# First layer of a two-layer model on one core: expert choice, prefix sums, positions and scatter issued one batch later, layer norm ahead of the squares

## The chip, the core and the metric

The kernel runs on 1 of the 8 cores of a Trainium2 chip. The metric is the device time of one execution in microseconds. Three executions of the kernel before took 2236.86, 2238.84 and 2248.63 us, median 2238.84. The engines are TensorE (PE; PEld is its weight load), VectorE (DVE), ScalarE (ACT), GpSimd (POOL) and SyncE (SP, which here only issues DMAs).

## What is computed

```python
xn = layernorm(x)                                   # x: 16 x 512 x 128, float32
x  = x + linear_attention(xn) + moe(xn)             # first layer
xn = layernorm(x)
x  = x + chunked_softmax_attention(xn) + rwkv_ffn(xn)   # second layer
...
# moe: 8 experts, top 2 of the softmax of xn @ router_w.T, weights renormalised,
# each expert relu(x @ w_fc.T)**2 @ w_proj.T, plus one shared MLP of the same form
# linear_attention: rope, phi = elu + 1, causal: num_t = q_t (sum_{s<=t} k_s v_s), divided by q_t sum k_s
```

The program computes its first-layer attention by blocks of 128 tokens: masked scores inside a block, sums of k v for the blocks before.

## The kernel before, in words

The first layer is a software pipeline over 16 batches of 512 tokens (`over_batches`: two batches written out, a hardware loop of six rounds with two batches each, two written out). Each engine has its own `body(b, first, last)`, and the engines meet by semaphores. Nothing plans the order: it is the order of the calls in those bodies. In body b the engines do the attention of batch b in four slices of four heads (`scores`, `evac_s` on ScalarE and `cut` on VectorE with `mask` on GpSimd, `attend`), the output of batch b-1 (`turn_y`, `project_out`, `residual`), the front of batch b+1 (`turn_xn`, `project_qk`, `rotate`, `project_v`, `turn_k`, `sum_states`, `states`), and the layer norm of batch b+2 (`ln_moments`, `ln_sqrt`, `ln`).

The choice of experts belongs to the front: for batch b+1, in body b,

- `router` (VectorE, L863 to L896): maximum of the logits, difference, exponential on ScalarE (`exp_router`, L620), sum, rank of each expert by comparing all pairs, `pickb` (top two) for TensorE, the two weights. 17 small operations, each waiting for the one before;
- `prefix` (TensorE, L1401): 14 small matmuls that count, for each token, the tokens before it that chose each expert, into bank W6;
- `slots` (VectorE, L909 to L925): the weights divided by their sum, the row of each choice from the counts and the running `fill`, as integers in `idx`;
- `store_route` (SP, L363 and L365): weights and rows to DRAM;
- `scatter` (GpSimd, L513): 8 indirect DMAs that write the rows of xn of the batch to the experts' queues in DRAM. For batch b they are issued in body b, three after the masks of slice 0, three after those of slice 1, two after those of slice 2.

The places that matter below:

- `ln` (L809 to L824) ends body b on VectorE, behind `square_h` and `slots`. Its last four operations write xn of batch b+2, and wait until the scatters of batch b have landed, since they read the same buffer.
- `turn_xn` (L1361) transposes xn into W6, which is shared by `turn_xn`, `turn_y`, `project_qk`, `project_v`, `turn_k`, `prefix` and `shared_fc`.
- `turn_oT(b, 0)` (L1483) waits for `residual` of batch b-1 (L962, semaphore xa_ready), since both use bank W7.
- `project_qk(b+1, 0)` (L1377) waits for the copy of yT on ScalarE (L630).
- `relu_h` (L636) on ScalarE and `square_h` (L957) on VectorE follow the four `shared_fc` matmul groups (L1505), two buffers each.

After the last batch VectorE makes a plan of tiles of 256 rows (L1036 to L1056), and the experts' tiles run, then the second layer. Both are the same before and after.

Of the kernel before, what the change touches and what calls it, by code (L numbers as in the profile page):

```python
# [16 lines left out]
NB = FF // 128  # L17
# [77 lines left out]
def build(nc, io, out):  # L95
    ctx = ExitStack()
    with ctx:
# [198 lines left out]
        def early(b, d):  # L296

            return b.less(d)
# [34 lines left out]
        def _(sp):  # L333
# [43 lines left out]
            def body(b, first, last):  # L377
                if not (b.known() is not None and b.known() + 2 >= B):
                    load_x(b + 2)
                if not first:  # L380
                    store_xa(b + -1)
                load_xr(b)
                if not last:
                    store_route(b + 1)

            store_route(Turn(0, 0))
            over_batches(sp, body)
# [101 lines left out]
        def _(pool):  # L489
# [27 lines left out]
            def body(b, first, last):  # L517
                for s in range(SHEETS):
                    for g in COPIED:
                        mask(b, s, g)  # L520
                    if s < SHEETS - 1:
                        scatter(b, range(3 * s, min(3 * s + 3, 2 * J)))

# [57 lines left out]
        def _(act):  # L581
# [69 lines left out]
            def front(n):  # L651
                exps(n)
                sheets_of_k(n)
                evac_v(n)
                evac_ktok(n)
                exp_router(n)

            def body(b, first, last):
                if not first:
                    evac_oT(b + -1, 3)  # L660
                evac_s(b, 0)
                if not last:
                    evac_xnT(b + 1)
                evac_s(b, 1)
                if not first:
                    evac_yT(b + -1)
                evac_oT(b, 0)
                evac_s(b, 2)
                if not last:
                    exps(b + 1)  # L670
                evac_oT(b, 1)
                if not last:
                    sheets_of_k(b + 1)
                evac_s(b, 3)
                if not last:
                    evac_v(b + 1)
                evac_oT(b, 2)
                if not last:
                    evac_ktok(b + 1)
                    exp_router(b + 1)  # L680
                if not (b.known() is not None and b.known() + 2 >= B):
                    ln_sqrt(b + 2)
                for k in range(NB):
                    relu_h(b, k)
# [105 lines left out]
        def _(dve):  # L790
# [174 lines left out]
            def front(n):  # L965
                rotate(n, 0)
                rotate(n, 1)
                feature(n)
                logits_out(n)
                states(n)  # L970
                router(n)
                slots(n)

            def body(b, first, last):
                cut(b, 0)
                if not first:
                    y_out(b + -1, 3)
                    normalise(b + -1)
                cut(b, 1)
                if not last:  # L980
                    rotate(b + 1, 0)
                cut(b, 2)
                if not first:
                    residual(b + -1)
# [12 lines left out]
                if not last:  # L997
                    states(b + 1)
                    router(b + 1)
                y_out(b, 2)  # L1000
                for k in range(NB):
                    square_h(b, k)
                if not last:
                    slots(b + 1)
                if more:
                    ln(b + 2)

# [344 lines left out]
        def _(pe):  # L1352
# [3 lines left out]
            def turn_xn(n, first_layer=True):  # L1356
                pe.wait_ge(xn_ready, n.at(J, J))
                if first_layer and not early(n, 1):
                    pe.wait_ge(prefix_read, n.at(1, 0))
                for j in range(J):  # L1360
# [3 lines left out]
            def project_qk(n, c):  # L1364
# [8 lines left out]
                else:  # L1373
                    pe.wait_ge(rot_cos, n.at(2, 1))
                    pe.wait_ge(rot_sin, n.at(2, 1))
                rhs = xnT[n.p][:, 1:T + 1]
                pe.matmul(W5[:, :], wqk[:, 2 * c, :], rhs, start=True, stop=True).then_inc(qk_ps, 1)  # L1377
# [12 lines left out]

            def prefix(n):

                pe.wait_ge(picked, n.at(1, 1))
                if early(n, 1):
                    pe.wait_ge(ktok_sb, n.at(1, 1))
                else:
                    pe.wait_ge(h_relu, n.at(NB, 0))
                for j in range(J + 1):
# [87 lines left out]
            def turn_y(b, last):  # L1486
                pe.wait_ge(y_ready, b.at(1, 1))
                if last:
                    pe.wait_ge(prefix_read, B)
                    pe.wait_ge(h_relu, b.at(NB, NB))  # L1490
                else:
                    pe.wait_ge(xnT_sb, (b + 2).at(1, 1))
# [5 lines left out]
            def shared_fc(b, k, last):  # L1498
# [4 lines left out]
                else:  # L1503
                    pe.wait_ge((state_sb, yT_sb)[k], (b, b + -1)[k].at(1, 1))
                pe.matmul((W5, W6)[k % 2][:, :], sfc[:, k * 128:(k + 1) * 128], xnT[b.p][:, 1:T + 1], start=True, stop=True).then_inc(fc_ps, 1)  # L1505
# [14 lines left out]
            def body(b, first, last):  # L1520
# [12 lines left out]
                if not first:  # L1533
                    project_out(b + -1)
                turn_oT(b, 0)
                if not last:
# [12 lines left out]
                for k in range(NB):  # L1549
                    shared_fc(b, k, last)  # L1550
                if not last:
                    prefix(b + 1)

# [7 lines left out]
            sum_states(n0)  # L1561
            prefix(n0)
            over_batches(pe, body)
# [276 lines left out]
```

## Time and profile before

| what | value |
| --- | --- |
| median of three executions | 2238.84 us |
| the profiled execution, its own time | 2259.64 us |
| its span (first to last instruction) | 2257.9 us |
| mean granted clock of TensorE | 0.812 |
| PE busy, share of the span | 1797.4 us, 80% |
| DVE busy | 1331.0 us, 59% |
| ACT busy | 938.0 us, 42% |
| POOL busy | 501.7 us, 22% |

The first layer takes the time up to about 775 us. A group of the profile's rows gives the start in us, the duration in us, the engine, the line of the kernel, the operation with its output and inputs (names of the program, `t`, `P`, `bank` stand for several buffers), the shape, and in brackets the idle time of the engine before it and who ended it. A granted clock of 1.00 is 2.4 GHz and 0.50 is 1.2 GHz. Durations of matmuls overlap, since they are pipelined: a group of 32 matmuls at 451.89 of 1.17 us ends where the next begins.

### The profile page before, as it was taken

What the parts mean: (1) busy time and instruction counts of PE and PEld (TensorE: products, weight loads), DVE (VectorE), ACT (ScalarE), POOL (GpSimd) and SP (SyncE); (2) the same over time, 40 slices, a digit from 0 to 9 for tenths busy, and PEclk for the clock granted to TensorE, in tenths of its full rate; (3) what the DMA queues carried; (4) which work ended last, traced back from release to release, by engine and by line L of the source; (5) the groups of instructions that cost most, each with busy time, mean ns of one, the idle gap of its engine ahead of it and who ended that gap; (6) DMA issues with size and microseconds to landing.
All of it is one profiled execution on the core that took longest, in us unless ns stands there. A gap on an engine that the chain in (4) does not pass through costs nothing.

```text
span 2257.9 us, 40845 instructions
## 1 busy us (share of the span) xinstructions
PE 1797.4 (80%) x13376; PEld 1062.4 (47%) x13376; DVE 1331.0 (59%) x3305; ACT 938.0 (42%) x1675; POOL 501.7 (22%) x517
## 2 busy tenths in 40 slices
PE   2788788888888699996478797777877778777796
PEld 1455455555555499996133343333433333333332
DVE  2666666665665444443565676666766666766563
ACT  2334334433443133332135454444544445444453
POOL 1443343344334111113211101111011110110000
PEclk9799989989988799998557876777767777677776
DMA  3010101011000366664333322233221332222200
GB/s 77 28 40 25 32 30 35 25 33 35 27 24 26 90 207 210 210 209 139 78 71 72 73 56 58 43 76 72 59 56 41 76 75 62 50 42 63 62 7 10
DMA packets 116987, 152.65 MB, mean 68 GB/s; under 512 B 29012, under 2 KB 81364, under 8 KB 112212
## 3 DMA queue, kind: packets, MB, share of 16 engines
q1 hardware_dynamic: 102920, 119.73, 21.7%
q0 software_dynamic: 13952, 31.48, 4.7%
q8 instruction: 61, 1.00, 0.2%
q14 instruction: 54, 0.44, 0.1%
HBM read 109.53 MB, written 41.62 MB: 67 GB/s over the span
## 4 chain that ended last, share of the span: by engine, by line
PE 56%; DVE 21%; DMA 9%; issue 8%; ACT 4%; SPq 1%; DVEq 0%; POOL 0%; POOLq 0%; ACTq 0%
PE bank L1640 7%; PE bank L1471 6%; PE bank L1594 6%; DVE nmax L1128 6%; PE bank L1585 6%; PE bank L1664 6%; DMA shift_d<-shift 5%; PE bank L1456 3%; PE bank L1453 3%; PE bank L1437 3%; PE bank L1516 3%; DMA QT<-shift_d 2%; PE bank L1483 2%; PE bank L1615 2%; PE bank L1377 2%
## 5 line engine op out<-in xcount | busy, mean ns | idle before, releaser
L1128 DVE TENSOR_REDUCE nmax<-bank 128x1 f32<-128x512 f32 (+3 forms) x704 | 432.5, 630 | 173.9 <-PE bank L1640 160.4
L733 ACT ACTIVATE P<-bank 128x512 f32<-128x512 f32 x640 | 369.0, 598 | 382.2 <-PE bank L1664 375.8
L1640 PE MATMUL bank<-KT,QT 76*128 76x512 bf16 (+3 forms) x1024 | 336.7, 389 | 107.7 <-DVE nmax L1128 84.6
L1664 PE MATMUL bank<-QT,KT 78*128 78x512 bf16 (+3 forms) x1024 | 318.8, 395 | 129.8 <-DMA QT<-shift_d 125.3
L1640 PEld LDWEIGHTS bank<-KT,QT 76*128 76x128 bf16 x1024 | 98.9, 114 | 337.9 <-DVE nmax L1128 286.4
L505 POOL TENSOR_TENSOR P<-P,tri 128x512 f32<-128x512 f32 x128 | 160.2, 1271 | 416.9 <-ACT P L643 416.7
L1664 PEld LDWEIGHTS bank<-QT,KT 78*128 78x128 bf16 x1024 | 117.4, 120 | 236.6 <-issue 113.7
L1471 PE MATMUL bank<-P,V 128*32 128x512 f32 (+3 forms) x2048 | 227.9, 529 | 0.0
L565 POOL DMA_DIRECT2D out<-xr x16 | 13.2, 822 | 740.9 <-DVE xr L1280 740.9
L1077 DVE TENSOR_TENSOR hT<-hr 128x512 f32<-128x512 f32 x144 | 99.6, 692 | 109.6 <-ACT hr L704 109.6
L704 ACT ACTIVATE hr<-bank 128x512 f32<-128x512 f32 x144 | 86.0, 597 | 167.6 <-PE bank L1585 167.6
L1594 PEld LDWEIGHTS bank<-P,hT 128*128 128x128 f32 x1152 | 140.4, 192 | 3.8
L544 POOL DMA_INDIRECT hT<-ys_d,idx x128 | 125.0, 977 | 76.4 <-issue 71.5
L1594 PE MATMUL bank<-P,hT 128*128 128x128 f32 x1152 | 140.5, 275 | 0.0
L1585 PE MATMUL bank<-P 128*128 128x256 f32 x576 | 139.9, 387 | 0.5 <-ACT P L699 0.5
L513 POOL DMA_INDIRECT xs_d<-xn,idx x128 | 126.6, 989 | 32.4 <-issue 32.0
L1361 PE MATMUL bank<-ident,xn 128*128 128x128 f32 x128 | 32.6, 404 | 113.4 <-DVE xn L824 113.4
L939 DVE COPY yb<-bank 128x144 f32<-128x144 f32 x128 | 38.5, 301 | 142.4 <-PE bank L1483 140.9
L626 ACT COPY oT<-bank 128x512 f32<-128x512 f32 x128 | 75.0, 586 | 101.5 <-PE bank L1456 60.4
L1456 PE MATMUL bank<-P,V 128*32 128x128 f32 x2048 | 116.8, 303 | 0.0
L1585 PEld LDWEIGHTS bank<-P 128*128 128x128 f32 x576 | 106.0, 194 | 12.8 <-ACT P L699 0.9
L530 POOL DMA_DIRECT2D ys_d<-P x72 | 52.2, 725 | 259.7 <-DVE P L1083 248.5
(207 smaller groups left out, 2750.6 us busy)
## 6 DMA issues: line engine op xcount, KB each, us to landing
P<-in_fc SPq DMA_DIRECT2D x72, 256.0 KB, 2.6
P<-in_proj SPq DMA_DIRECT2D x72, 256.0 KB, 2.9
QT<-parts_d SPq DMA_DIRECT2D x96, 192.0 KB
parts_d<-parts SPq DMA_DIRECT2D x32, 384.0 KB, 2.6
P<-xs_d SPq DMA_DIRECT2D x72, 128.0 KB, 2.2
ys_d<-P POOLq DMA_DIRECT2D x72, 128.0 KB, 2.7
KT<-parts_d SPq DMA_DIRECT2D x64, 128.0 KB
KT<-parts_d SPq DMA_DIRECT2D x32, 192.0 KB
```

The source lines that it names most:

```text
L505: nc.gpsimd.tensor_tensor(blocks, blocks, tri[:, :, :], ALU.mult).then_inc(a_masked, 1)
L513: nc.gpsimd.indirect_dma_start(xs_d[:, :], bass.IndirectOffsetOnAxis(ap=idx[n.p][:, k:k + 1], axis=0), xn[n.p][:, k % J, :], None).then_in ...
L544: nc.gpsimd.indirect_dma_start(ya[n.p][:, k, :], None, ys_d[:, :], bass.IndirectOffsetOnAxis(ap=idx[n.p][:, k:k + 1], axis=0)).then_inc(ga ...
L733: nc.scalar.activation(P[s % 2][:, u, :], bank[k % 2][:, :], ACT.Exp, scale=float(DH) ** -0.5).then_inc(s_sb, 1)
L1077: nc.vector.tensor_tensor(hT[:, t.p % 2, 2 * k:2 * k + 2, :], h, h, ALU.mult).then_inc(e_sq, 1)
L1128: nc.vector.tensor_reduce(nmax[:, j, h:h + nh], bank[2 + k % 2][:, 0:nh * w].rearrange("p (h w) -> p h w", h=nh), AX.X, ALU.max, negate=Tr ...
L1456: ins = pe.matmul(OT[32 * g:32 * g + 32, tile], V[b.p][:, j, G * s + g, :], P[s % 2][:, g, tile], start=(j == 0), stop=True, skip_group_ch ...
L1471: ins = pe.matmul(OT[32 * g:32 * g + 32, 128 * kb:T], V[b.p][:, kb, G * s + g, :], P[s % 2][:, u, c:c + n], start=(k == 0), stop=(k == J - ...
L1585: ins = pe.matmul(w[:, i * GT:(i + 1) * GT], wfc[t.p][:, c * 128:(c + 1) * 128], xgT[t.p % 2], start=True, stop=True)
L1594: ins = pe.matmul(bank[6 + t.p % 2][:, c * 128:(c + 1) * 128], hT[:, t.p % 2, k, c * 128:(c + 1) * 128], wpj[t.p][:, k, :], start=(k == 0) ...
L1640: ins = pe.matmul(bank[2 + k % 2][:, i * w:(i + 1) * w], QT[n.p][0:MROWS, h, j * 128:(j + 1) * 128], KT[n.p][0:MROWS, h, 0:w], start=True, ...
L1664: ins = pe.matmul(bank[k % 2][:, c:c + n], KT[b.p][0:SROWS, h, 128 * kb:128 * kb + 128], QT[b.p][0:SROWS, h, 128 * kb:T], start=True, stop ...
```

## The change

Everything of the expert choice of batch b+1 that stood in body b now stands in body b+1, and is written with b. On VectorE `router(b)` comes behind `cut(b, 1)`, `slots(b)` behind `cut(b, 2)` and ahead of `residual(b-1)`; on ScalarE `exp_router(b)` behind `evac_s(b, 1)`; on TensorE `prefix(b)` behind `project_out(b-1)`; on SP `store_route(b)` behind `load_xr(b)`; on GpSimd all 8 scatters behind the masks of slice 2. `ln(b+2)` moves up, behind `states(b+1)`, ahead of the last `y_out` and the squares. On ScalarE `evac_ktok(b+1)` now precedes `evac_oT(b, 2)`. Waits for bank W6 are rewritten for the new order. No arithmetic changes.

```diff
@@ SP
                 load_xr(b)
-                if not last:
-                    store_route(b + 1)
-
-            store_route(Turn(0, 0))
+                store_route(b)
@@ POOL
                     for g in COPIED:
                         mask(b, s, g)
-                    if s < SHEETS - 1:
-                        scatter(b, range(3 * s, min(3 * s + 3, 2 * J)))
+                    if s == SHEETS - 2:
+                        scatter(b, range(2 * J))
@@ ACT, front and body
                 evac_ktok(n)
-                exp_router(n)
...
                 evac_s(b, 1)
+                exp_router(b)
                 if not first:
                     evac_yT(b + -1)
...
-                evac_oT(b, 2)
                 if not last:
                     evac_ktok(b + 1)
-                    exp_router(b + 1)
+                evac_oT(b, 2)
@@ DVE, front and body
                 states(n)
-                router(n)
-                slots(n)
...
                 cut(b, 1)
+                router(b)
                 if not last:
                     rotate(b + 1, 0)
                 cut(b, 2)
+                slots(b)
                 if not first:
                     residual(b + -1)
...
                     states(b + 1)
-                    router(b + 1)
+                if more:
+                    ln(b + 2)
                 y_out(b, 2)
                 for k in range(NB):
                     square_h(b, k)
-                if not last:
-                    slots(b + 1)
-                if more:
-                    ln(b + 2)
@@ PE
             def turn_xn(n, first_layer=True):
                 pe.wait_ge(xn_ready, n.at(J, J))
-                if first_layer and not early(n, 1):
-                    pe.wait_ge(prefix_read, n.at(1, 0))
+                if first_layer and not early(n, 2):
+                    pe.wait_ge(h_relu, (n + -1).at(NB, 0))
+                elif first_layer and not early(n, 1):
+                    pe.wait_ge(ktok_sb, n.at(1, 0))
...
                     pe.wait_ge(rot_sin, n.at(2, 1))
+                    if not early(n, 1):
+                        pe.wait_ge(prefix_read, n.at(1, 0))
...
-            def prefix(n):
+            def prefix(n, last):
                 pe.wait_ge(picked, n.at(1, 1))
-                if early(n, 1):
-                    pe.wait_ge(ktok_sb, n.at(1, 1))
+                if not last:
+                    pe.wait_ge(rot_sin, (n + 1).at(2, 1))
                 else:
-                    pe.wait_ge(h_relu, n.at(NB, 0))
+                    pe.wait_ge(yT_sb, n.at(1, 0))
...
                     project_out(b + -1)
+                prefix(b, last)
                 turn_oT(b, 0)
...
                     shared_fc(b, k, last)
-                if not last:
-                    prefix(b + 1)
```

TensorE before, from the last shared matmuls of one batch into the next (`ident,xn` is turn_xn, `pickb` prefix, `P,QT` scores, `sfc` shared_fc, `oT` turn_oT):

```order
L1505 MATMUL bank<-xnT,sfc 128x512 [waits h_relu] x2
L1401 MATMUL bank<-pickb,before 128x8 [waits h_relu,picked]
L1401 MATMUL bank<-pickb,before 128x8 x13
L1437 MATMUL bank<-P,QT 128x128 [waits a_sb,a_cut,phi,k_sheets]
L1437 MATMUL bank<-P,QT 128x128 x15
L1483 MATMUL bank<-ident,oT 128x128 [waits y_sb,oT_sb]
L1483 MATMUL bank<-ident,oT 128x128 x3
L1361 MATMUL bank<-ident,xn 128x128 [waits prefix_read,xn_ready]
```

TensorE after, in the middle of a batch, from the end of project_out (`wo,yT`) to the attention of slice 1; prefix now stands here, and nothing stands between the shared matmuls and the scores:

```order
L1514 MATMUL bank<-wo,yT 128x128
L1399 MATMUL bank<-pickb,before 128x8 [waits rot_sin,picked]
L1399 MATMUL bank<-pickb,before 128x8 x13
L1481 MATMUL bank<-ident,oT 128x128 [waits xa_ready,y_sb,oT_sb]
L1481 MATMUL bank<-ident,oT 128x128 x3
L1375 MATMUL bank<-xnT,wqk 128x512 [waits prefix_read,rot_sin,rot_cos]
L1376 MATMUL bank<-xnT,wqk 128x512
```

The prefix matmuls moved from the end of the batch before to between project_out and turn_oT, and wait there for the choice and for the first rotation of the next batch.

VectorE after, from the cut of slice 2 to the copy of the first outputs:

```order
L931 TENSOR_TENSOR P<-bank,tri 128x512 [waits a_ps]
L906 TENSOR_SCALAR psum_<-psum_ 128x4
L907 RECIPROCAL psum_<-psum_ 128x4 [waits slots_step]
L911 TENSOR_TENSOR wts<-p,psum_ 128x8 [waits slots_step]
L916 TENSOR_TENSOR pos<-bank,fill 128x32 [waits prefix_read,prefix_ps]
L918 TENSOR_TENSOR fill<-fill,bank 128x8 [waits slots_step]
L919 TENSOR_TENSOR prod<-pick,pos 128x64
L921 TENSOR_REDUCE slotf<-prod 128x8 [waits slots_step]
L922 CAST idx<-slotf 128x8 [waits slots_step]
L959 TENSOR_TENSOR xr<-xr,bank 128x512 [waits xr_loaded0,proj_ps]
L936 COPY yb<-bank 128x4x36 [waits oTT_ps]
```

Slots moved in between the cut and the residual, and its middle waits for the prefix matmuls of the same batch.

## Rows read from the trace of the kernel before

**Rows 1.** Waits of PE, 94 to 715 us: total, times, longest.
```profile
PE bank L1361 <- DVE xn L824: 47.4, 12, 4.2
```
**Rows 2.** Stretches: length, PE, PEld, DVE, ACT, POOL busy, then PEclk, DMA, GB/s.
```profile
94.60:714.50 619.90, 524.07 (x5562) 349.20 (x5558) 389.44 (x1029) 249.05 (x432) 250.28 (x224) 0.91 0.10 30
...
721.30:724.60 3.30, 1.23 (x34) 1.03 (x33) 3.20 (x7) 1.50 (x4) 2.96 (x3) 1.00 0.05 5
724.70:728.10 3.40, 3.40 (x24) 1.95 (x24) 1.03 (x2) 0.66 (x2) 2.77 (x4) 0.50 0.15 43
```
**Rows 3.** Timeline of PE, a back-edge and the shared matmuls of the next batch.
```profile
412.57 2.09 PE L1437 MATMUL bank<-P,QT 32*128 32x128 f32 x32 [3.92 <-issue]
...
446.78 3.80 PE L1505 MATMUL bank<-xnT,sfc 128*128 128x512 f32 x8
```
**Rows 4.** Timeline of DVE, end of the same batch.
```profile
443.77 0.61 DVE L844 TENSOR_TENSOR P<-bank,own 128x432 f32<-128x432 f32 x1 [1.78 <-PE bank L1421]
...
444.99 0.18 DVE L878 TENSOR_REDUCE psum_<-pr 128x4 f32<-128x32 f32 x1 [0.30 <-ACT pr L620]
...
448.84 0.16 DVE L896 TENSOR_TENSOR psum_<-p 128x4 f32<-128x4 f32 x1
...
453.93 1.11 DVE L814 SCALAR_TENSOR_TENSOR std<-mv,std 128x4 f32<-128x4 f32 x1
...
460.00 0.69 DVE L949 TENSOR_TENSOR y<-yb,rden 128x512 f32<-128x512 f32 x1
```
**Rows 5.** Timeline, end of the last batch: shared matmuls, last square.
```profile
747.42 3.80 PE L1505 MATMUL bank<-xnT,sfc 128*128 128x512 f32 x8
...
751.89 0.69 DVE L957 TENSOR_TENSOR hT<-hr 128x512 f32<-128x512 f32 x1 [0.17 <-ACT hr L636]
```
**Rows 6.** Timeline of DVE, start of the last batch.
```profile
721.04 1.29 DVE L934 TENSOR_TENSOR P<-bank,tri 128x512 f32<-128x512 f32 x2
...
723.45 1.08 DVE L949 TENSOR_TENSOR y<-yb,rden 128x512 f32<-128x512 f32 x1
```
**Rows 7.** Timelines of DVE and PE: slots behind prefix, and project_out to turn_oT.
```profile
409.33 0.19 DVE L919 TENSOR_TENSOR pos<-bank,fill 128x32 f32<-128x32 f32 x1
...
410.14 0.17 DVE L925 CAST idx<-slotf 128x8 int32<-128x8 f32 x1
...
429.12 0.39 PE L1517 MATMUL bank<-wo,yT 128*128 128x128 f32 x2
...
429.64 0.69 DVE L962 TENSOR_TENSOR xr<-xr,bank 128x512 f32<-128x512 f32 x1 [2.71 <-PE bank L1517]
...
430.47 0.63 PE L1483 MATMUL bank<-ident,oT 128*128 128x128 f32 x4 [0.97 <-DVE xr L962]
```
**Rows 8.** POOL: timeline, then all scatters: ns min/median/max, and us to landing.
```profile
453.74 2.50 POOL L505 TENSOR_TENSOR P<-P,tri 128x512 f32<-128x512 f32 x2 [11.90 <-ACT P L643]
...
457.71 0.96 POOL L513 DMA_INDIRECT xs_d<-xn,idx  x1 [0.30 <-issue]
...
L513 POOL DMA_INDIRECT xs_d<-xn,idx x128: 954/959/1459, 65.0 to 738.1; - x128
...
DMA to landing us min/median/max: 2.2/2.3/3.6
```
**Rows 9.** Timeline of DVE, batch 0: router begins, moments of batch 1 begin.
```profile
53.89 0.18 DVE L874 TENSOR_REDUCE lmax<-lg 128x4 f32<-128x32 f32 x1
...
60.02 0.86 DVE L799 BATCH_NORM_STATS2 stats<-xt 128x6 f32<-128x128 f32 x4
```
**Rows 10.** Timeline of PE, last batch: first turn_oT, attention of slice 3.
```profile
736.02 0.63 PE L1483 MATMUL bank<-ident,oT 128*128 128x128 f32 x4 [0.87 <-DVE xr L962]
...
744.75 0.42 PE L1456 MATMUL bank<-P,V 128*32 128x128 f32 x8
```
**Rows 11.** Timeline of ACT, batch 0: a table load, and the exponential it is for.
```profile
33.35 1.28 ACT L599 ACT_TABLE_LOAD   x1
...
39.19 0.63 ACT L599 ACTIVATE ee<-t 128x512 f32<-128x512 f32 x1 [4.56 <-DVE t L837]
```

More of the change, by code:

```diff
@@ L1488, in turn_y @@
                 if last:
-                    pe.wait_ge(prefix_read, B)
                     pe.wait_ge(h_relu, b.at(NB, NB))
@@ L1503, in shared_fc @@
                 else:
-                    pe.wait_ge((state_sb, yT_sb)[k], (b, b + -1)[k].at(1, 1))
+                    pe.wait_ge((state_sb, prefix_read)[k], b.at(1, 1))
                 pe.matmul((W5, W6)[k % 2][:, :], sfc[:, k * 128:(k + 1) * 128], xnT[b.p][:, 1:T + 1], start=True, stop=True).then_inc(fc_ps, 1)
@@ L1561, in _ @@
             sum_states(n0)
-            prefix(n0)
             over_batches(pe, body)
```

## The prediction

> **What bounds the kernel now.** I read the waits of TensorE over the batches of the first layer first, then the two engines' timelines of one batch, then the clock. The change touches nothing after 780 us, so all of it must be found between 30 and 780 us. TensorE (PE) is the busiest engine there, and it has one large wait: the transposes of the normalised rows (L1361) wait 12 times, 47.4 us in total, for VectorE (DVE) to write xn [rows 1]. DVE is late because it runs one chain ahead of it: router, squares of the shared MLP, slots, layer norm. Each such gap is followed by a stretch at 1.2 GHz instead of 2.4: the mean granted clock over the fourteen batches from the E (below) of batch 0 to that of batch 14 is 0.91 [rows 2], so 0.18 of the time, 8 us of a batch, is at the lower level. A batch is 44.28 us long (619.90/14).
>
> I call E the moment at which TensorE issues the first shared matmul of batch b (446.78), and T the moment at which it starts the first turn_oT of a batch (430.47) [rows 3, 7]. In the batch of these rows y of batch b is ready at 460.69 and its transposes can start at 460.8, E+14.0 [rows 3, 4]. Two of the loop's back-edges differ: there TensorE stands idle for nothing that the profile names, 3.92 us before 412.57 [rows 3], and xn is ready by then.
>
> **The batch after the change.** At its end, DVE goes from the masking of states (ends 444.38) to the layer norm, 1.0 us of small operations and 1.1 us for xn, and is done at E+0.1. The square root it needs follows the copy of k on ScalarE; its table load (1.28) and itself (0.3) should end at about 444.2, just in time. The squares then go at the pace of ScalarE's relus. The last batch shows this pace, since its end has no router: last square done 5.16 us after its E [rows 5]. The present end of a batch is hardly slower (5.27), so the squares gain 0.1 only. What goes is what follows them: slots and layer norm in front of the first two cuts.
>
> - TensorE issues the first scores at E+3.8 (they take 3.80 [rows 3]), without the wait for the last relu and the 14 prefix matmuls, then turn_oT and turn_xn, to E+6.15.
> - DVE cuts at E+5.17. From the first cut to y ready it took 3.49 us in the last batch [rows 6], with the reciprocal and the mask of GpSimd (POOL) at the same relative place as they will have now. y is ready at E+8.7, and turn_y starts at E+8.75. Against E+14.0 that is **-5.25 us**. TensorE stands 1.1 us before turn_y.
> - DVE cuts again to E+9.9 and starts the router. Alone it takes 0.7 us to the exponential and 4.0 from L878 to L896 [rows 4]. POOL's second mask pair runs then (E+8.3 to E+10.8). The small L814, with two SBUF inputs, takes 1.11 us while L505 runs (453.74 to 456.24 [rows 4, 8]), where its like take 0.16. So L875 ends at E+11.0, the exponential at E+11.3, the router at E+15.3.
> - ScalarE's exponential table load moves here. It isn't held by the semaphore: at 33.35 it ran at once, and the exponential waited until 39.19 [rows 11]. So it costs nothing here; were it held, 1.3 us. The copy of yT behind it ends at E+11.9; project_qk needs it at E+12.1. Cover of 0.2 us, the thinnest of all.
> - The rotation starts at E+15.3 instead of E+13.2, and takes 2.65; the cut of slice 2 ends at E+19.2, the three first operations of slots at E+19.85. TensorE ends project_out at E+19.4 and prefix at E+19.85. Slots takes 0.98 us from there (409.33 to 410.31 [rows 7]), the residual 0.7, and turn_oT starts at E+21.8. It needs the residual done (xa_ready), and slots now stands in front of the residual. Before, it was 0.96 us from the end of L1517 to turn_oT [rows 7]; now it is 2.35: **+1.4 us**, the prefix matmuls among them.
> - From T to the next E it is 16.3 us as before [rows 3, 7].
> - POOL: 8 scatters in one burst, 1.26 us each [rows 8], 10.1 us from T-0.9 on, then the last mask pair (2.5): done at T+11.7. attend(3) wants it 2.7 us before E [rows 5, 10], T+13.6. Slack 1.9. The last scatter lands 2.3 us (at most 3.6) after its issue [rows 8], by T+12.9; the layer norm writes xn at T+14.9. Nothing waits.
> - SP: store_route now comes behind load_xr of the same batch. slots_ready(b) comes before xa_ready(b-1), on which the queue stands anyway, so it adds no wait; load_x is issued some 20 us earlier than now.
>
> A batch without any low clock is thus 38.1 us against 42.0 (14.0 + 11.65 + 16.3) now. The real one is 44.28, so low clock costs 2.3 us of a batch.
>
> **The sum.** 12 batch ends save 5.25 (63.0); the two back-edges with an idle stretch of their own save only the relu wait and the prefix, 1.35 each (2.7): the stretch begins that much earlier. The end of batch 14 has no xn wait; y is ready at 724.53, E+10.0 [rows 2, 6], and comes to E+8.7: 1.3. Fifteen times slots in front of the residual: +21. At the start, router and slots of batch 0 no longer stand ahead of the moments of batch 1: from 53.89 to 60.02, -6.1 [rows 9]. In the last batch nothing of a next batch lies between T and attend(3), which came 8.7 us after T [rows 10], and the burst and mask need T+11.7: +3.0. The plan behind its squares shifts with it. Sum: -63.0 -2.7 -1.3 +21.0 -6.1 +3.0 = **-49 us**.
>
> **The clock** I take as unchanged in length, and this is where I chose. The 4 us gap goes, but gaps of 1.1 us before turn_y and 1.9 us before turn_oT come. Batch 15 shows two gaps together (PE busy 1.23 of 3.30 us), and the next 3.40 us ran at 0.50 [rows 2]: shorter gaps than 4 us can lower the clock. The present 0.96 us before turn_oT did not. The new 1.9 lies between. Bounds: no low stretch at all, 2.3 us a batch more gained, -35 us; or one more stretch of 6.8 us at half speed in each batch, up to 3.4 us each, +51.
>
> The Trainium skill (TensorE: Matmul & The Clock Gate, "Why this matters for your kernels") blames only a longer idle gap between bursts for such a drop. By it the clock would stay at 2.4 GHz with both new gaps, and the result would be that of the second rival. The trace speaks partly against it, by the row of batch 15.
>
> The profiled execution lasted 2259.6 us (span 2257.9), 20.8 more than the median 2238.8. -49 on its own time gives 2211; on the median **2190 us**.
>
> **The rivals.**
> 1. *The new gaps lower the clock once more in each batch.* For it: the row of batch 15. Against: work between the gaps is dense. Half of the batches with a second stretch of 3.4 us: +25, 2215 us; all of them, 2241.
> 2. *The clock stays high.* All gaps are halved, the longest goes. -49 -35: 2155 us.
> 3. *The new waits eat more than worked out*: the exponential is late, yT with it, then router, rotation, slots. Each us there is a us of TensorE. With 1.3 for a held table load, and the same again on the way through the router to the residual: +2.6 a batch, 39: 2229 us.
> 4. *Slower: the burst holds the mask.* If each scatter took what the slowest took, 1.46 us, plus 0.30, the burst would last 14.1 us; the mask would end at T+15.6, 2.0 us after attend(3) wants it, and the gap would bring a low stretch of 3.4. 5.4 us x 15 = +81: 2271 us. The wait begins at 1.5 us a scatter; the sign turns at 3.3 us lost per batch. Against: the median of 128 scatters is 0.959 [rows 8], with DVE busy beside them.
> 5. *Slower: DVE starves the burst.* A scatter that first waited for one of DVE's operations of 0.69 us [rows 7] would make the burst 5.5 us longer, 3.6 more than the slack, and the clock adds 3.4: 7.0 x 15 = +105 -49, 2295 us. Against: the 128 scatters ran beside rotations and cuts, and half of them took 0.959 or less [rows 8].
>
> The Trainium skill (SBUF — State Buffer, "SBUF: two separate sides") states this last mechanism: GpSimd can't write the descriptors of its DMAs while DVE runs an operation that takes both ports. It gives some 3100 against 620 ns for one; at that factor no batch would fit, and by an estimate from it the kernel would be some 200 us slower. The trace has no such scatter, so it gets 0.02.
>
> **How the numbers follow.** Forecast 0.55 (own range 2172 to 2208: +-1.2 us a batch). Rival 1 0.13, rival 2 0.12, rival 3 0.12, rivals 4 and 5 0.03 and 0.02; 0.03 for a new wait of which nothing is seen. A measurement of this kernel tells 0.5%, 11 us, from no change. Faster by more than that: forecast, rival 2, most of rivals 1 and 3, 0.86. Within: part of rivals 1 and 3, 0.07. Slower: rivals 4 and 5 and most of the unseen wait, 0.07. The range leaves out the slow cases and the far end of rival 1: 2153 to 2226 us.
>
> **What would show it.** Right: the wait of L1361 for xn gone from the waits of PE; turn_xn near E+5.6; E to E 40 to 41 us; a wait before turn_oT of 1.9 us put down to the residual, a wait of 1.1 before turn_y; scatters in one run of 10 us that ends before the mask of slice 3 is wanted; first scores near 53.5 us. Wrong: the sum of the new waits of PE above 4 us a batch; a clock of more than 0.95 or under 0.88 over the batches (rivals 2 and 1); attend(3) waiting for POOL; project_qk waiting for yT.

## The result, and the profile after

The changed kernel takes **2314.64 us** (median of 4 runs, 2308.49 to 2322.53); the kernel before, run beside it, 2243.74 us (4 runs, 2236.86 to 2256.49). The ratio is 1.031, with a 95% interval from 1.025 to 1.037: slower by 71 us, where 49 us less were forecast. The forecast and its whole range are wrong.

The waits of TensorE (PE) and of the engines it feeds, from 90 to 760 us of the changed kernel (engine, line, what was waited for: us in total, times, longest):

```profile
PEld bank L1435 <- issue: 68.7, 114, 3.6
DVE P L931 <- PE bank L1435: 68.3, 13, 6.5
ACT oT L624 <- remote: 67.1, 14, 6.4
...
PE bank L1481 <- DVE xr L959: 33.2, 14, 2.5
PE bank L1435 <- issue: 32.4, 59, 2.8
...
PE bank L1491 <- DVE y L946: 14.5, 14, 1.1
```

The wait of [rows 1] is gone, as forecast: no line of TensorE waits for xn. The two new gaps are there too, 1.1 us before turn_y and 2.5 (forecast 1.9) before turn_oT. But there are rows that nothing in the forecast answers to. The scores of slice 3 (L1435) stand still for "issue", that is for nothing that the profile names. VectorE (DVE) waits 13 times for these late scores, 5.3 us on average. And ScalarE (ACT) waits 14 times, 4.8 us on average and up to 6.4, for work that TensorE had started long before; "remote" stands for a semaphore whose giver the profile doesn't find. One batch on TensorE, in two pieces:

```profile
439.08 3.80 PE L1502 MATMUL bank<-xnT,sfc 128*128 128x512 f32 x8
442.81 1.17 PE L1435 MATMUL bank<-P,QT 32*128 32x128 f32 x32
444.12 0.65 PE L1481 MATMUL bank<-ident,oT 128*128 128x128 f32 x4
444.61 0.60 PE L1357 MATMUL bank<-ident,xn 128*128 128x128 f32 x4
...
447.84 0.65 PE L1491 MATMUL bank<-ident,y 128*128 128x128 f32 x4 [1.06 <-DVE y L946]
...
461.67 0.63 PE L1481 MATMUL bank<-ident,oT 128*128 128x128 f32 x4 [2.49 <-DVE xr L959]
...
466.27 0.42 PE L1454 MATMUL bank<-P,V 128*32 128x128 f32 x8
466.63 0.88 PE L1435 MATMUL bank<-P,QT 32*128 32x128 f32 x10
467.95 0.26 PE L1435 MATMUL bank<-P,QT 32*128 32x128 f32 x1 [0.45 <-issue]
468.66 0.49 PE L1435 MATMUL bank<-P,QT 32*128 32x128 f32 x3 [0.44 <-issue]
469.38 0.26 PE L1435 MATMUL bank<-P,QT 32*128 32x128 f32 x1 [0.23 <-issue]
470.09 0.39 PE L1435 MATMUL bank<-P,QT 32*128 32x128 f32 x2 [0.44 <-issue]
470.81 0.37 PE L1435 MATMUL bank<-P,QT 32*128 32x128 f32 x1 [0.34 <-issue]
471.52 1.08 PE L1435 MATMUL bank<-P,QT 32*128 32x128 f32 x4 [0.35 <-issue]
472.94 1.01 PE L1435 MATMUL bank<-P,QT 32*128 32x128 f32 x10 [0.33 <-issue]
...
485.57 0.70 PE L1502 MATMUL bank<-xnT,sfc 128*128 128x512 f32 x1
```

Up to T (461.67) this is the forecast: turn_xn at E+5.5 (5.6 forecast), turn_y at E+8.76 (8.75). Then the scores of slice 3, 32 small matmuls that take 1.17 us at 442.81, take 7 us: from 467.5 on TensorE starts one to a few, then nothing until the next point of a grid 0.71 us wide (467.95, 468.66, 469.38, 470.09 ...), until about 473. From T to the next E it is 23.9 us instead of 16.3.

The row of ACT in the same stretch, and POOL's run of scatters:

```profile
473.03 0.59 ACT L624 COPY oT<-bank 128x512 f32<-128x512 f32 x1 [6.36 <-remote]
```
```profile
461.60 1.01 POOL L511 DMA_INDIRECT xs_d<-xn,idx  x1 [3.78 <-DVE idx L922]
...
466.71 0.96 POOL L511 DMA_INDIRECT xs_d<-xn,idx  x1 [0.30 <-issue]
467.97 0.96 POOL L511 DMA_INDIRECT xs_d<-xn,idx  x1 [0.30 <-issue]
...
470.50 0.96 POOL L511 DMA_INDIRECT xs_d<-xn,idx  x1 [0.31 <-issue]
```

The last attend matmul of slice 1 was started before 466.63, and what it produced was copied by ACT at 473.03 only. POOL itself keeps its pace, 8 scatters at 1.26 us, though the first comes at T-0.1 and not at T-0.9 as forecast. In this batch the first gap begins at 467.5, 5.9 us after the first scatter, and the last one ends at 472.94, 11.3 us after it. I count all stretches below from the first scatter of the run.

Over 14 batches, E to E is 47.82 us (44.28 before): 22.71 from E to T (28.02 before, 21.8 forecast), and 25.11 from T to E (16.26 before, 16.3 forecast). So the whole loss, 8.85 us a batch, lies between T and E. About half of it is the stall: over these 14 batches the scores of slice 3 take 5.5 us on average, from their first start to the start of what follows, where they took 1.1 before. Much of the rest is a lower clock. In nine of the 14 batches it falls behind the 2.5 us in front of turn_oT, so that these scores start at T+6.3 or later where it was T+5.0. And it falls again behind the stall (length, then busy time of PE, PEld, DVE, ACT and POOL, then the granted clock, the DMA share and GB/s):

```profile
466.60:473.00 6.40, 3.80 (x30) 2.17 (x27) 0.73 (x2) 0.07 (x1) 3.84 (x4) 0.80 0.17 58
473.00:479.80 6.80, 6.80 (x61) 4.88 (x61) 2.84 (x12) 4.55 (x9) 2.49 (x2) 0.69 0.00 0
479.80:485.50 5.70, 5.13 (x58) 3.64 (x56) 2.98 (x12) 2.55 (x4) 0.00 (x0) 1.00 0.00 0
```

### The profile page after: what moved, and what is told of

The parts are those of the page before. It is cut to its first block, busy times and chain, and to the rows that moved or that the text cites. A ratio compares the mean times of both kernels' runs of the same rounds, so it can differ in the third digit from the quotient of the medians.

```text
span 2317.7 us, 40825 instructions
## 1 busy us (share of the span) xinstructions
PE 1851.6 (80%) x13376; PEld 1099.3 (47%) x13376; DVE 1344.7 (58%) x3305; ACT 933.6 (40%) x1675; POOL 510.7 (22%) x517
## 4 chain that ended last, share of the span: by engine, by line
PE 54%; DVE 21%; issue 10%; DMA 8%; ACT 4%; SPq 1%; DVEq 0%; POOLq 0%; POOL 0%; ACTq 0%
PE bank L1635 7%; PE bank L1469 6%; PE bank L1659 6%; PE bank L1589 6%; PE bank L1580 5%; DVE nmax L1122 5%; DMA shift_d<-shift 5%; PE bank L1454 4%; PE bank L1451 3%; PE bank L1502 3%; PE bank L1435 3%; PE bank L1481 2%; DVE P L931 2%; DMA QT<-shift_d 2%; PE bank L1610 2%
## 5 line engine op out<-in xcount | busy, mean ns | idle before, releaser
L503 POOL TENSOR_TENSOR P<-P,tri 128x512 f32<-128x512 f32 x128 | 168.4, 1335 | 408.4 <-ACT P L641 408.4
L1435 PE MATMUL bank<-P,QT 32*128 32x128 f32 x2048 | 112.2, 308 | 41.1 <-issue 34.0
L931 DVE TENSOR_TENSOR P<-bank,tri 128x512 f32<-128x512 f32 x128 | 82.0, 681 | 99.4 <-PE bank L1435 70.6
L1481 PE MATMUL bank<-ident,oT 128*128 128x128 f32 x512 | 100.1, 329 | 39.3 <-DVE xr L959 35.7
L1454 PE MATMUL bank<-P,V 128*32 128x128 f32 x2048 | 124.7, 317 | 3.6 <-issue 3.6
```

Source lines behind the costliest of these rows:

```text
L503: nc.gpsimd.tensor_tensor(blocks, blocks, tri[:, :, :], ALU.mult).then_inc(a_masked, 1)
L931: nc.vector.tensor_tensor(P[s % 2][:, g, :].rearrange("p (j c) -> p j c", c=128), bank[g][:, :].rearrange("p (j c) -> p j c", c=128), tri[ ...
L1435: ins = pe.matmul(bank[g][:, tile], kS[b.p][quad, s, tile], qf[b.p][quad, tile], start=True, stop=True)
L1454: ins = pe.matmul(OT[32 * g:32 * g + 32, tile], V[b.p][:, j, G * s + g, :], P[s % 2][:, g, tile], start=(j == 0), stop=True, skip_group_ch ...
L1481: ins = pe.transpose(W7[:, j * 128:(j + 1) * 128], oT[s % 2][:, j * 128:(j + 1) * 128], ident[:, :])
```

## The experiments

The theory after this reading: **the run of eight scatters stalls TensorE**, though nothing there depends on them. Rivals: the five transfers of SP (SyncE), which now fall together with the burst; the place in the program (slots and norm beside the scores of slice 3).

**The burst alone, in the kernel before.** Everything stays as before, but all eight scatters go behind the masks of slice 0:

```diff
-                    if s < SHEETS - 1:
-                        scatter(b, range(3 * s, min(3 * s + 3, 2 * J)))
+                    if s == 0:
+                        scatter(b, range(2 * J))
```

> The kernel before, with one edit: all 8 scatters of a batch stand in one run behind the masks of slice 0 (before: 3, 3 and 2). Burst theory: TensorE issues almost nothing from about 6.3 to 11.4 us after the first scatter of a run of 8, wherever the run stands; here that falls into attend(0), project_qk and scores of slice 2 of every batch, so 4 to 5 us a batch are lost and the median is 2295 to 2330 us. Traffic theory (the run only hurts beside SP's three transfers of 256 KB, which stand at another place here): no stall, 2240 to 2255 us. Place theory (TensorE stops at scores of slice 3 for a wait of its own): no stall either.

Measured: 2320.82 us, ratio to before 1.036 [1.030, 1.043]. This one edit, with no router, slots or norm moved, costs 78 us and brings the stall into other code. One batch, whose first scatter was issued at 258.1 (PE, then ACT, then DVE):

```profile
265.38 0.38 PE L1437 MATMUL bank<-P,QT 32*128 32x128 f32 x2 [0.45 <-issue]
265.68 0.69 PE L1516 MATMUL bank<-spj,hT 128*128 128x128 f32 x2
266.81 0.40 PE L1516 MATMUL bank<-spj,hT 128*128 128x128 f32 x2 [0.44 <-issue]
268.24 0.40 PE L1516 MATMUL bank<-spj,hT 128*128 128x128 f32 x2 [1.04 <-issue]
268.96 0.38 PE L1516 MATMUL bank<-spj,hT 128*128 128x128 f32 x2 [0.32 <-issue]
269.66 0.79 PE L1517 MATMUL bank<-wo,yT 128*128 128x128 f32 x2 [0.32 <-issue]
```
```profile
269.83 1.07 ACT L643 COPY P<-bank 128x512 f32<-128x512 f32 x2 [5.30 <-remote]
```
```profile
265.39 0.69 DVE L832 TENSOR_TENSOR t<-bank,rope 128x512 f32<-128x512 f32 x1 [0.72 <-remote]
266.19 0.69 DVE L835 TENSOR_TENSOR t<-t 128x512 f32<-128x512 f32 x1
266.92 0.43 DVE L837 TENSOR_SCALAR t<-t 128x512 f32<-128x512 f32 x1
269.91 1.29 DVE L934 TENSOR_TENSOR P<-bank,tri 128x512 f32<-128x512 f32 x2 [2.57 <-remote]
```

The same grid, 6.9 to 11.6 us after the first scatter, now in the projections (L1516). The rows of DVE tell who is held: between 265.4 and 267.4 it goes through three operations, each behind the semaphore of the one before, at its usual pace. Only what comes from TensorE is late: the scores' last two matmuls started at 265.38, and ACT and DVE got them at 269.8 and 269.9. The place in the program falls as a cause.

**SP's transfers held back**, in the changed kernel: ahead of its three stores and loads of a batch, SP waits until the scores of slice 3 are done.

```diff
+                sp.wait_ge(a_ps, b.at(H, H))
                 if not first:
                     store_xa(b + -1)
                 load_xr(b)
```

> The changed kernel, with one wait more on SP: its stores and loads of a batch go out only when the scores of slice 3 are done, so none of the 256 KB transfers runs beside the 8 scatters before TensorE's stall. Burst theory: the stall stays, 6.3 to 11.4 us after the first scatter, 2300 to 2325 us. Traffic theory: the stall goes, and the median is 2190 to 2225 us.

Measured: 2315.36 us, ratio 1.036 [1.029, 1.043]. The stall is unchanged (T to E 25.1 us), and SP's transfers now start only behind it. SP's traffic is not it.

**The burst split**, in the changed kernel, four scatters behind the masks of slice 2 and four behind those of slice 3:

```diff
-                    if s == SHEETS - 2:
-                        scatter(b, range(2 * J))
+                    if s >= SHEETS - 2:
+                        scatter(b, range(J * (s - SHEETS + 2), J * (s - SHEETS + 3)))
```

> The changed kernel, with 4 scatters behind the masks of slice 2 and 4 behind those of slice 3. Burst theory: no run is longer than 5 us, so TensorE doesn't stall in scores of slice 3; but the last scatter lands some 19 us after turn_oT(b, 0), 4 us after the layer norm wants to write xn, so the squares and the first cut come about 2 us late: 2215 to 2235 us. Place theory: the stall stays and the late layer norm adds to it, over 2330 us.

Measured: 2200.88 us, ratio 0.983 [0.977, 0.989]: 114 us less than the changed kernel, and 42 us less than the kernel before. Run once more later, beside the last two kernels below:

> The split kernel once more, beside the swap and beside the kernel before on the same chip: 2195 to 2210 us.

Measured: 2194.79 us, ratio 0.976 [0.970, 0.983]. The scores of slice 3, and one of the landings that DVE now waits for (the norm of the batch after next may overwrite xn only when all eight are done):

```profile
450.05 1.17 PE L1435 MATMUL bank<-P,QT 32*128 32x128 f32 x32
...
461.32 3.80 PE L1502 MATMUL bank<-xnT,sfc 128*128 128x512 f32 x8
```
```profile
462.63 1.11 DVE L821 TENSOR_SCALAR xn<-xt,mv,rstd 128x128 f32<-128x128 f32 x4 [2.83 <-DMA xs_d<-xn,idx]
```

The first scatter of this batch was issued at 443.52, so the scores of slice 3 begin 6.5 us after it, and they are back at 1.17 us. So it is in most batches. In two or three of fourteen they begin about 5 us after it, and there they still take 1.5 to 1.7 us where 1.1 is usual: four in a row are not quite free either, which the last experiment shows better. The 2.83 us of DVE delay nothing that TensorE waits for: its transposes of xn follow at 466.96. So it did better than the 2215 to 2235 us expected.

**A short pause in the burst.** Eight small memsets between the fourth and the fifth scatter, which lengthen that spacing from 1.26 to 1.9 us:

```diff
                 for k in ks:
+                    for c in range(8 if k in (4,) else 0):
+                        nc.gpsimd.memset(fhn[c][:, :, :], 0.0)
                     nc.gpsimd.indirect_dma_start(
```

> The changed kernel, with eight memsets of 64 columns (about 1.25 us in all) on POOL between the 4th and the 5th scatter. Burst theory, if a pause lets TensorE go on: the stall goes or shrinks to under 2 us, 2190 to 2230 us. If only the total counts (8 scatters within some 12 us), or in the traffic and place theories: the stall stays at 4 to 6 us, 2305 to 2330 us.

Measured: 2307.71 us, ratio 1.031 [1.025, 1.038]. The stall stays, its gaps lie between 6.0 and 11.7 us. In the split kernel the fifth scatter is issued 9 us after the fourth; 1.9 us is not enough.

**How many may follow each other?** Five and three, then six and two, in place of four and four:

```diff
-                        scatter(b, range(J * (s - SHEETS + 2), J * (s - SHEETS + 3)))
+                        scatter(b, range(5) if s == SHEETS - 2 else range(5, 2 * J))
```

> After, with five scatters behind the masks of slice 2 and three behind those of slice 3. In the split 4 and 4 no matmul stalled (2200.9 us); with all eight the stall began about 6.3 us after the first scatter, when the sixth was issued. Theory 1 (the stall begins with the sixth scatter of a burst): five are free, scores of slice 3 spread over 0.9 us in every batch, time 2195 to 2210 us. Rival (any burst of more than four brings it, from its last scatters on): scores of slice 3 spread over 2 us or more, 2225 us or more.

> After, with six scatters behind the masks of slice 2 and two behind those of slice 3. Theory 1 (the stall begins with the sixth scatter and lasts until the last of the burst has landed, 2.05 us after its issue): a stall of about 2 us per batch, from 6.3 to about 8.6 us after the first scatter, a third of the 5 us with all eight; time 2201 + 14 x 2 to 3 = 2230 to 2245 us. Rival A (only the number of eight, or what the seventh and eighth do): no stall, 2195 to 2210 us. Rival B (a stall once begun runs its whole course of 5 us): 2290 us or more.

Measured: 2211.84 us with five (ratio 0.984 [0.981, 0.987]), 2 us above the range of theory 1, and 2241.27 with six (0.9995 [0.996, 1.003]). The stall of one batch with six, first scatter at 417.38:

```profile
424.10 0.99 PE L1435 MATMUL bank<-P,QT 32*128 32x128 f32 x13
425.32 0.26 PE L1435 MATMUL bank<-P,QT 32*128 32x128 f32 x1 [0.24 <-issue]
426.04 0.93 PE L1435 MATMUL bank<-P,QT 32*128 32x128 f32 x18 [0.45 <-issue]
```

| scatters in the run | gaps in the scores of slice 3, counted from the first scatter | T to E, mean of 14 | time |
|---|---|---|---|
| 4 (then 4) | none; the scores mostly begin at 6.5 | 17.7, 17.5 | 2200.9, 2194.8 |
| 5 (then 3) | mostly none; in one of 14 batches up to 7.2 us | 18.3 | 2211.8 |
| 6 (then 2) | first begins at 5.6 to 7.7 us, last ends at 8.6 | 20.4 | 2241.3 |
| 8 | first begins at 5.9 to 8.3 us, last ends at up to 11.4 | 25.1 | 2314.6 |

The times nearly follow the first theory of the two expectations, and so does the end of the stall: it lasts until about 2 us after the last scatter of the run is issued, which is about when that scatter lands (2.3 us after its issue, [rows 8]). "Five are free" is not so: the scores of slice 3 take 1.4 to 1.6 us in most batches instead of 1.1, and 2.9 in the one in which they begin 5 us after the first scatter. And that the stall begins with the sixth is not shown. Where it begins in these rows hangs on when the scores begin and how many of them get through before the first gap (13 in the rows above, 10 in the changed kernel). The last experiment moves the scores forward and settles it.

**All eight later, beside wide matmuls.** The split kernel, with the layer norm behind the squares and all scatters behind the masks of slice 3:

```diff
-                    if s >= SHEETS - 2:
-                        scatter(b, range(J * (s - SHEETS + 2), J * (s - SHEETS + 3)))
+                    if s == SHEETS - 1:
+                        scatter(b, range(2 * J))
```

> After, with the layer norm behind the squares and all eight scatters behind the masks of slice 3, so that the stretch from 6.3 to 11.4 us after the first scatter falls on other code: the end of the eight wide shared matmuls (128x512, 0.45 us each, about 2.5 instructions per us) and what follows them, instead of the scores (32 matmuls and 32 weight loads in 0.9 us). Theory 1 (in the stretch TensorE gets only a few instructions per 0.71 us, and does no harm where it needs few): the wide shared matmuls keep their spacing of 0.45 us even where they fall into the stretch, and the 0.71-us grid shows only in scores and turns. Rival (TensorE is held by its data or its results, so that each matmul is slower): the wide matmuls that fall into the stretch are spaced by more than 0.7 us too. The time, since the last scatter lands about 5 us later than in the split kernel and the norm waits for it: 2265 + 14 x 2 to 5 us = 2290 to 2340 us.

Measured: 2359.27 us, ratio 1.050 [1.045, 1.055], above the 2290 to 2340 expected. The wide matmuls keep their spacing, as theory 1 had it, but neither theory foresaw what else the rows show (PE, then ACT; first scatter at 447.38):

```profile
452.08 1.99 PE L1502 MATMUL bank<-xnT,sfc 128*128 128x512 f32 x4
459.37 3.78 PE L1502 MATMUL bank<-xnT,sfc 128*128 128x512 f32 x4 [5.30 <-ACT hr L634]
```
```profile
458.72 1.09 ACT L634 ACTIVATE hr<-bank 128x512 f32<-128x512 f32 x2 [9.41 <-remote]
```

The four wide matmuls start 0.43 us apart and are done by 454.1, 6.7 us after the first scatter. The first relu needs only the first two of them (one matmul of the kernel), and waits for a semaphore that this matmul itself increments; ACT is idle and has waited for nothing else since 449.3, but starts at 458.72, 11.3 us after the first scatter. So **what TensorE has to tell ACT arrived some 5 us late**, and TensorE itself had nothing left to start after 454.1. (The profile models the ends of matmuls, so it can't tell whether the matmul ended late or only its signal did. In the rows of b_burst later matmuls started before the signal of the earlier ones arrived.) The stall thus has two halves: TensorE's signals are held until its end, and beside that TensorE starts new matmuls only every 0.71 us where it has many to start. The kernel that has only wide matmuls there suffers nearly as much, because the next ones wait for the relu: 94 us more than the same kernel with the scatters split (2264.8 us, below), where the changed kernel loses 114.

**The layer norm's place, alone and taken back.** In the kernel before, only the norm of the batch after next moved ahead of y_out of slice 2 and the squares:

```diff
                     states(b + 1)
                     router(b + 1)
+                if more:
+                    ln(b + 2)
                 y_out(b, 2)
...
                     slots(b + 1)
-                if more:
-                    ln(b + 2)
```

> Before, with only the layer norm of the batch after next moved ahead of the third output step and the squares on VectorE; scatters and slots stay. Theory (the wait of the transposes for xn, 4.2 us in 12 batches, is what the edit takes away, and it is independent of the router's move): 2243 - 12 x 4.2 = about 2193 us; some of it may come back since the slots and the squares behind end about 4 us later (scatters of the next batch): 2190 to 2210 us. Rival (the layer norm can only come forward if the router's and slots' steps leave that place too, since VectorE is then late with the squares): 2230 us or more.

Measured: 2215.68 us, ratio 0.987 [0.980, 0.993], somewhat above the 2190 to 2210 of the theory. The wait for xn is gone, but the prefix matmuls, which need the last relu, now wait for it three times as long (before 13.4, 15, 1.1):

```profile
PE bank L1401 <- ACT hr L636: 42.5, 15, 3.3
```

29 of the 47 us come back so, since the squares, and with them the relus, start later behind router and norm. And the split kernel with its norm put back behind the squares:

```diff
-                if more:
-                    ln(b + 2)
                 y_out(b, 2)
                 for k in range(NB):
                     square_h(b, k)
+                if more:
+                    ln(b + 2)
```

> After, with the scatters split 4 and 4, and the layer norm put back behind the squares. Theory (with router and slots gone from that place the norm waits there for nothing that the second four scatters do not hold back anyway): the norm ends about 2 us later than in the split kernel and the transposes of xn wait 0 to 2 us: 2201 to 2225 us. Rival (the place of the layer norm is what gives the whole gain): back to 2235 us or more.

Measured: 2264.8 us, ratio 1.010 [1.007, 1.014]: 64 us more than the split kernel, and my expectation was wrong. I had priced the squares by DVE's own time. They go at the pace of the relus, and those at the pace of the shared matmuls, so a norm behind the squares is a norm behind the end of all shared matmuls:

```profile
467.19 0.66 PE L1357 MATMUL bank<-ident,xn 128*128 128x128 f32 x4 [3.77 <-DVE xn L821]
```
```profile
PE bank L1357 <- DVE xn L821: 44.5, 12, 3.8
```

The wait of [rows 1] is back in full, with the low clock behind it (0.89 over 90 to 760 us, against 0.94 in the split kernel). So the move of the router alone (with the scatters four and four) loses some 20 us, that of the norm alone wins 27, and both without the burst win 42 to 54: each part clears the place that the other needs.

**One swap more.** In the split kernel TensorE waits 2.3 to 2.5 us before turn_oT for the residual. The second query and key projection of the next batch needs only the prefix to be read:

```diff
-                turn_oT(b, 0)
                 if not last:
                     project_qk(b + 1, 1)
+                turn_oT(b, 0)
```

> The split kernel with one swap on TensorE: the second pair of query and key projections of the next batch ahead of the first turn of oT. In the split kernel TensorE waits 2.5 us per batch in front of that turn for VectorE's residual, while the projection's own inputs (the prefix read on VectorE) are there about 0.9 us earlier. Theory: the projection starts 0.9 us earlier and the wait shrinks by that: 14 x 0.9 = 12 us less than the split kernel, 2185 to 2200 us. Rival: the turn comes 1.9 us later, and the output step on VectorE and the rotation queued behind it lose what was won: 2201 us or more.

Measured: 2183.99 us (4 runs, 2183.06 to 2194.03), ratio to before 0.973 [0.969, 0.977], the fastest of all; the split kernel in the same comparison 2194.79. The two intervals overlap, so the times do not settle that the swap is worth its 11 us. The rows show two effects that nearly cancel. The wait before turn_oT (35.0 us in 15 times in the split kernel) is now one of half the size before the projection, no second wait stands behind it, and the clock over 90 to 760 us is 0.97:

```profile
PE bank L1375 <- DVE fill L918: 15.6, 14, 1.2
```

But the scores of slice 3 now begin 3.8 us after the first scatter instead of 6.5, and this is one batch of them, first scatter of four at 436.75:

```profile
440.52 0.79 PE L1435 MATMUL bank<-P,QT 32*128 32x128 f32 x13
441.66 0.26 PE L1435 MATMUL bank<-P,QT 32*128 32x128 f32 x1 [0.35 <-issue]
442.38 0.93 PE L1435 MATMUL bank<-P,QT 32*128 32x128 f32 x18 [0.45 <-issue]
```

**A run of four stalls TensorE too**, with gaps from 4.6 to 5.7 us after the first scatter, in thirteen batches; the scores take 2.6 to 3.2 us there instead of 1.1, and ACT's wait for TensorE's signal is back 13 times, up to 1.2 us. The stall opens before a fifth scatter would be issued (5.1 us). It is the same grid: wherever the scatters follow each other at 1.26 us, the gaps end about 5.7, 6.4, 7.1, 7.8, 8.5 us and so on after the first, and the last one at 5.7 with four, 7.2 with five, 8.6 with six and 11.4 with eight, 1.4 us later for each scatter more. The split kernel escaped it because its scores begin mostly behind 5.7 us. A batch is 39.80 us long on average here and 40.05 in the split kernel run beside it, 3.5 us in all; of the 9 us by which the last E comes earlier, 5.7 arise in the last batch, in which the swap changes nothing. The same swap with at most three scatters in a row was not tried. Nothing is seen with three: in the kernel before, scores that ran from 2.9 to 4.0 us after the first scatter took their 1.17 us.

## Why the prediction was wrong

**The step that failed** is the line on POOL, "8 scatters in one burst, 1.26 us each ... Nothing waits", and with it "From T to the next E it is 16.3 us as before". I had the scatter's own numbers nearly right: its spacing, and the end of the burst before the mask is due (the last ends at T+9.8 in the batch shown, forecast T+9.2). What I did not ask is what eight in a row do to an engine that has no dependency on them. The trace before never has more than three in a row (3, 3 and 2 per batch), so its 128 scatters could not show it, and I used them as evidence far outside what they cover. T to E became 25.1 us instead of 16.3. Undoing that one step (the split) takes 7.4 us out of T to E and, since E to T was 0.4 longer in that execution, 7.0 out of a batch; 15 times that is 105 to 111 us, and 114 were measured. Rivals 4 and 5 had the right place and sign, and wrong mechanisms: POOL was not late, and attend(3) never waited for its mask. DVE did not starve the burst either, the scatters keep a median of 962 ns (959 in [rows 8]). The true case sat in the 0.03 for "a new wait of which nothing is seen".

**What held**, point by point:
- The batch end: turn_y at E+8.76 against 8.75; the wait for xn gone; the thin cover before project_qk held (it starts at E+12.0).
- The table load of the exponential cost TensorE nothing: the copy of yT behind it ends at E+11.8, forecast 11.9.
- E to T: 22.71 on average against 21.8, mostly 22.4 to 22.6. The rotation explains it: in each of these 14 batches its L834 takes 1.38 us beside POOL's mask, where I had left it at 0.43:

```profile
456.73 1.38 DVE L834 TENSOR_SCALAR t<-t 128x512 f32<-128x512 f32 x1
```

- The slots in front of the residual: the wait before turn_oT is 2.3 to 2.5 us, forecast 1.9.
- The clock: I took it as unchanged. In the split kernel it is better on the whole (0.94 against 0.91), since the long gap before turn_xn is gone. But T to E is still 17.7 and not 16.3, because a stretch at 1.2 GHz often follows the gap before turn_oT, as rival 1 had it: from 396 to 400 us the split kernel, run the second time, was granted 0.57 behind a gap of 2.49, and the swapped kernel 1.00 from 395 to 400 behind one of 1.17. Both effects nearly cancel. Rival 2, in which the new gaps leave the clock at 2.4 GHz, did not come.
- The start: first scores at 51.75 us (58.24 before, 53.5 forecast). Of these 6.5 us the E of batch 0 kept only 1.8 in the split kernel (92.8 against 94.58).
- The sum: without the burst the kernel takes 2201 and 2195 us against the 2190 forecast, and a batch 40.8 and 40.05 us against 40.4. That is closer than the terms deserve: E to T and T to E came out longer than forecast, and the gain in clock paid for it.

The Trainium skill (SBUF — State Buffer, "SBUF: two separate sides") has DVE hold up the descriptors of GpSimd's DMAs; no run here shows it, 128 scatters beside DVE's work took 957 to 1449 ns. Its lock between the two engines is seen the other way round, in DVE operations that last over 1 us beside POOL's mask.

## What to carry to other kernels

A statistic of an operation holds for the pattern in which it occurred: before a change makes runs of something that used to be spread out, look for the longest run in the trace, and treat a longer one as unmeasured, for engines that do not depend on it too. Spread software-made DMAs over the free places of POOL: here three in a row cost nothing that the traces show, and four cost 1.5 us wherever dense small matmuls fell on the stretch from 4.6 to 5.7 us after the first. A place where the matmuls escape the stretch is not proof that there is no stretch; the next reordering can move them into it. And when work is queued behind a chain that another engine paces, its price is the end of that chain, not the busy time of what stands before it.

## What was new about the hardware

- Indirect scatters of 128 rows, issued every 1.26 us, hold TensorE from about 4.6 us after the first (seen with four; with more in a row the dense matmuls mostly came later) until about 2 us after the last is issued: to 5.7 us with four in a row, 7.2 with five, 8.6 with six, 11.4 with eight. In this stretch matmuls start on a 0.71-us grid counted from the first scatter, and what TensorE has done reaches ACT and DVE late, with eight up to 6.4 us. DVE goes on at its usual pace meanwhile, and POOL too. With three in a row nothing is seen.
- How soon it shows depends on TensorE's own work: 10 to 30 of the small matmuls get through before the first gap, and four wide ones without any.
- Between the fourth and the fifth scatter 1.9 us from issue to issue do not help, 9 us do; nothing in between was tried.
- Why TensorE is held is open. The instructions and the signals of TensorE may share something with the descriptors of the scatters, but no run here shows that path. Whether the number of scatters, of rows or of bytes decides wasn't tried either. The eight gathers in a row of layer 2 show no such gaps in TensorE's timeline; it runs fewer and wider instructions there, but that was not tested.
